# Moving a layer's tail into the next stage, a wait for padding to its reader, and a queue's loads to other places

## The reference

```python
x = _L0(x, ctx, mask)      # cross attention, 16 heads of 16, gated residual
x = _L1(x, ctx)            # RWKV block: recurrence over tokens, 32 heads of 8, then a channel mix
x = _L2(x, ctx, mask)      # grouped-query attention, 32 query heads, 8 key/value heads of 8
x = _L3(x, ctx, ctx)       # two wide cross attentions (16 heads of 128) and an MLP of 1024
```

```python
out = out @ Wo + bo
x = out + hidden_state
mu = jnp.mean(x, axis=-1, keepdims=True)
var = jnp.var(x, axis=-1, keepdims=True)
return (x - mu) * jax.lax.rsqrt(var + EPS) * gamma + beta
```

## Time and profile before

| | |
|---|---|
| median of 3 runs | 1333.27 us (1333.21 to 1338.27) |
| profiled execution, its own time | 1336.37 us |
| span of the profile | 1334.6 us |
| PE busy | 1229.8 us (92%) |
| DVE busy | 807.0 us (60%) |
| ACT busy | 536.7 us (40%) |
| POOL busy | 180.2 us (13%) |
| mean granted TensorE clock | 0.96 |

### The profile page before, as it was taken

The page is one execution under the profiler, slowest core; times in us unless marked ns, Lnnn a source line. Parts: engine busy times, 40 slices in busy tenths (PEclk is TensorE's granted clock), DMA queues, the critical chain, the costliest instruction groups (busy, mean ns, idle before and its releaser), DMA issues.

```text
span 1334.6 us, 17906 instructions
## 1 busy us (share of the span) xinstructions
PE 1229.8 (92%) x6056; PEld 862.5 (65%) x6064; DVE 807.0 (60%) x2386; ACT 536.7 (40%) x1233; POOL 180.2 (13%) x397
## 2 busy tenths in 40 slices
PE   7769788898989787999999699999999999999999
PEld 4347555464555343444443488888888888888887
DVE  4434337586958336787785466666666666666620
ACT  3235343343534324555455343344343434334432
POOL 3122013022212111102011100000000000000000
PEclk9779899899989879999999899999999999999999
DMA  7454623101111535543524733030303030500000
GB/s 224 129 146 127 199 74 117 71 32 64 40 56 49 151 134 153 175 130 118 170 77 140 255 130 119 9 127 0 127 0 127 0 127 0 190 1 1 1 9 24
DMA packets 100652, 127.59 MB, mean 96 GB/s; under 512 B 6737, under 2 KB 78577, under 8 KB 98321
## 3 DMA queue, kind: packets, MB, share of 16 engines
q1 hardware_dynamic: 99936, 126.14, 29.1%
q10 hardware_dynamic: 624, 0.30, 0.1%
HBM read 79.33 MB, written 46.79 MB: 95 GB/s over the span
## 4 chain that ended last, share of the span: by engine, by line
PE 77%; DMA 8%; DVE 5%; ACT 3%; SPq 2%; issue 2%; POOL 2%; ACTq 0%; POOLq 0%; DVEq 0%
PE J L2448 8%; PE J L2466 8%; PE TT L2456 8%; PE S L2422 4%; PE OO L1077 4%; PE TT L2432 4%; PE OO L2422 4%; PE OO L1074 3%; PE J L324 2%; PE J L1077 2%; PE J L1343 2%; PE OO L2666 2%; PE S L634 2%; DMA km<-query_parts 2%; PE J L1074 2%
## 5 line engine op out<-in xcount | busy, mean ns | idle before, releaser
L2524 ACT ACTIVATE PT<-TT 128x512 f32<-128x512 f32 x128 | 76.5, 597 | 281.2 <-PE TT L2432 281.2
L2595 DVE TENSOR_SCALAR QK<-J,cols 128x256 f32<-128x256 f32 x126 | 61.0, 484 | 69.6 <-PE J L2448 69.6
L2559 POOL COPY On<-probs 128x8 f32<-128x8 f32 x128 | 29.1, 227 | 475.3 <-DVE probs L2584 446.0
L2584 DVE TENSOR_SCALAR probs<-probs,inv 128x257 f32<-128x257 f32 x256 | 79.1, 352 | 4.5
L1077 PE MATMUL OO<-ctxT,weights_a 128*128 128x512 f32 x136 | 69.9, 638 | 12.3 <-SPq L308 9.5
L2432 PE MATMUL TT<-ident,probs 128*128 128x128 f32 x512 | 76.9, 273 | 1.7 <-DVE probs L2584 1.7
L1074 PE MATMUL OO<-weights_a,ctxT 128*128 128x512 f32 x136 | 67.8, 622 | 9.8 <-SPq L308 6.1
L2432 PEld LDWEIGHTS TT<-ident,probs 128*128 128x128 f32 x512 | 63.8, 141 | 15.7 <-DVE probs L2584 3.0
L2590 DVE COPY km<-TT 128x256 f32<-128x256 f32 x128 | 54.2, 423 | 31.0 <-PE TT L2456 30.8
L970 DVE CUSTOM_DVE_ANT_0 mask_b<-S,weights_a 128x256 f32<-128x256 f32 x64 | 24.6, 422 | 70.0 <-PE S L634 69.8
L2576 DVE TENSOR_REDUCE maxes<-S 128x1 f32<-128x257 f32 x128 | 48.4, 420 | 30.4 <-PE S L2422 30.4
(11 more groups left out here) (413 smaller groups left out, 2704.4 us busy)
## 6 DMA issues: line engine op xcount, KB each, us to landing
wide_keys<-weights_a SPq DMA_DIRECT2D x64, 256.0 KB, 2.1
wide_values<-weights_a SPq DMA_DIRECT2D x56, 256.0 KB, 2.0
query_parts<-weights_a SPq DMA_DIRECT2D x48, 192.0 KB, 2.8
weights_a<-wide_keys SPq DMA_DIRECT2D x16, 512.0 KB, 7.2
weights_a<-wide_values SPq DMA_DIRECT2D x16, 512.0 KB, 8.4
early<-wide_keys SPq DMA_DIRECT2D x16, 512.0 KB, 8.2
early<-wide_values SPq DMA_DIRECT2D x16, 512.0 KB, 8.7
weights_a<-key_parts SPq DMA_DIRECT2D x16, 288.0 KB
```

Source lines behind the costliest of these rows:

```text
L2524: act.activation(PT[:, n % 2, :], T0[:, :], ACT.Copy).then_inc(pt3_ready, 1)
L2584: ins = dve.tensor_scalar(P_[n % 2][:, qt, :], P_[n % 2][:, qt, :], inv[:, qt, n % 32:n % 32 + 1], None, ALU.mult)
L2595: dve.tensor_scalar(QK[:, n % 2, 0, 0:S], J0[:, 0:S], head_cols(f"bq{a + 1}")[:, h:h + 1], float(DIM3) ** -0.5, ALU.add, ALU.mult).then_in ...
```

## The change

1. The tail of L2's last batch leaves stage 2. PE projects it into bank J1 in place of O0. In the wide stream DVE starts with the two additions, takes statistics and variance at item 0 and centres at item 1; POOL takes the root at item 1, applies gamma at item 2 and beta at item 3. PE's first `add_head`, which overwrites J1, waits for the first addition (`last2_read`), and DVE waits for beta at item 7, before `xn` is written again.
2. PE no longer waits for `pad_ready`; DVE waits for it just before `fetch_values(0)`.
3. In the first layer the copies of step 3 are issued at `at == 1`, with no wait for maxima and so directly behind those of step 2.
4. The table `later` is put in another order: nothing at step 0; mixing weights from step 1 on; `L2_o` and the `rows` table at step 5, ahead of the eight L1 weights, which go to steps 5 to 7. The wait for the eight stores moves with them to `L2_o`.

```diff
--- before.py
+++ after.py
@@ -581,9 +581,11 @@
                 n, i = at // CHUNKS0, at % CHUNKS0
                 b = n // 2
                 if i == 5 and 0 <= n + 1 < STEPS0:
-                    if n < 1:
+                    if n < 0:
                         sp.wait_ge(max0_rows_ready, n + 2)
                         spread0(sp, n + 3)
+                if at == 1:
+                    spread0(sp, 3)
                 if n >= 0 and i >= 6:
                     load_rest(n, 2 * (i - 6), 2 * (i - 6) + 2)
                 if n == 4:
@@ -1432,7 +1434,6 @@
                             pe.wait_ge(max_rows_ready, n + 2)
                         flip_on(n - 1, J0)
 
-                pe.wait_ge(pad_ready, 1)
                 for at in range(-LEAD2, LAST):
                     n, i = at // CHUNKS2, at % CHUNKS2
                     if at >= 0:
@@ -1468,7 +1469,7 @@
                 flip_od(STEPS2 - 1, T0)
                 flip_on(STEPS2 - 1, T1)
                 project_head(pe, 0, 1, 1)
-                project_out(B - 1, O0)
+                project_out(B - 1, J1)
                 bias_rows_pe(pe, 0, S0)
                 meet(pe, "pe")
 
@@ -1608,8 +1609,6 @@
                         front_pool_first(3, pool, 0)
                 pool.wait_ge(max_taken, STEPS2 * SLOTS2)
                 bias_rows_pool(pool, 0)
-                root(B - 1)
-                scale_out(B - 1)
                 meet(pool, "pool")
 
             def dve_program(dve):
@@ -1683,7 +1682,6 @@
                 def centre_out(b):
                     centre(dve, lambda t: xn[:, t, :], xn, own_rstd, rstd2_ready, b + 1, normed2)
 
-                dve.wait_ge(pad_ready, 1)
                 for at in range(-LEAD2, LAST):
                     n, i = at // CHUNKS2, at % CHUNKS2
                     if at == 0:
@@ -1693,6 +1691,7 @@
                     for m, f in fills_of(at):
                         take_maxima(m, f)
                     if at == 2 - LEAD2:
+                        dve.wait_ge(pad_ready, 1)
                         fetch_values(0)
                     if n % 2 == 0 and i == 2 and n // 2 + 1 < B and n >= 0:
                         fetch_values(n // 2 + 1)
@@ -1715,10 +1714,6 @@
                 fetch_q(dve, 0, 0, 0)
                 dve.wait_ge(x_flipped, 1)
                 fetch_q(dve, 0, 1, 1)
-                add_out(B - 1, O0)
-                add_bias()
-                variance()
-                centre_out(B - 1)
                 meet(dve, "dve")
 
             programs["pe"].append(pe_program)
@@ -2385,6 +2380,8 @@
         q3_done, q3_ready = names3("q3_done"), names3("q3_ready")
         var3_ready, rstd3_ready, xn3_ready = names3("var3_ready"), names3("rstd3_ready"), names3("xn3_ready")
         h3_flipped, h3_ready, weights_cleared = names3("h3_flipped"), names3("h3_ready"), names3("weights_cleared")
+        last2_read, last2_var, last2_rstd, last2_normed, last2_step, last2_scaled = (names3(n) for n in (
+            "last2_read", "last2_var", "last2_rstd", "last2_normed", "last2_step", "last2_scaled"))
         FRONT_AT = 8
         ROWS_AT = 3 * HEADS3 + 12
 
@@ -2462,6 +2459,8 @@
                     pe.wait_ge(av3_ready, n + 1)
                     if h == 0 and g >= 1:
                         pe.wait_ge(out3_fetched, g)
+                    if n == 0:
+                        pe.wait_ge(last2_read, 1)
                     for qt in range(TQ):
                         pe.matmul(J1[:, qt * S:(qt + 1) * S], avT[:, n % 2, qt * P:(qt + 1) * P], wide[a][1][:, h, :],
                                   start=(h == 0 and qt == 0), stop=False)
@@ -2560,6 +2559,16 @@
                         .then_inc(weights3_ready, 1)
                     if h == 6:
                         take_root(pool, next_rstd.rearrange("p t o -> p (t o)"), var3_ready, rstd3_ready, g + 1)
+                    if n == 1:
+                        take_root(pool, own_rstd.rearrange("p t o -> p (t o)"), last2_var, last2_rstd, 1)
+                    if n == 2:
+                        gamma = row("L2_xattn_gamma").unsqueeze(1).to_broadcast([P, TQ, C])
+                        pool.wait_ge(last2_normed, 1)
+                        pool.tensor_tensor(xn[:, :, :], xn[:, :, :], gamma, ALU.mult).then_inc(last2_step, 1)
+                    if n == 3:
+                        beta = row("L2_xattn_beta").unsqueeze(1).to_broadcast([P, TQ, C])
+                        pool.wait_ge(last2_step, 1)
+                        pool.tensor_tensor(x_of(B - 1), xn[:, :, :], beta, ALU.add).then_inc(last2_scaled, 1)
                     if n == HEADS3:
                         bias_rows_pool(pool, 1)
                     if h == 0 and g in (B - 1, B):
@@ -2605,6 +2614,10 @@
                     dve.wait_ge(out3_fetched, g + 1)
                     dve.tensor_tensor(x_of(g % B), x_of(g % B), xs[:, :, :], ALU.add)
 
+                bo2 = row("L2_xattn_bo").unsqueeze(1).to_broadcast([P, TQ, C])
+                dve.tensor_tensor(xn[:, :, :], two(J1), x_of(B - 1), ALU.add).then_inc(last2_read, 1)
+                dve.wait_ge(last2_read, 1)
+                chain.link(dve.tensor_tensor(xn[:, :, :], xn[:, :, :], bo2, ALU.add))
                 maxima(0)
                 divide(0)
                 for n in range(ITEMS3):
@@ -2621,6 +2634,13 @@
                         divide(n + 1)
                     if h == 2 and g >= 1:
                         add_out(g - 1)
+                    if n == 0:
+                        take_stats(dve, chain, lambda t: xn[:, t, :])
+                        take_variance(dve, chain, EPS2, own_rstd, last2_var)
+                    if n == 1:
+                        centre(dve, lambda t: xn[:, t, :], xn, own_rstd, last2_rstd, 1, last2_normed)
+                    if n == 7:
+                        dve.wait_ge(last2_scaled, 1)
                     following = x_tok, (g + 1) % B
                     if h == 4:
                         take_stats(dve, chain, tile_of(*following))
@@ -2784,9 +2804,10 @@
             layer1 = load_layer1(split_k)
             table = (rows[:, :, :], "rows", "rows", d["rows"].rearrange("(o r) n -> o r n", o=1)
                      .to_broadcast([P, len(ROWS), C]))
-            later = {0: [table] + layer1[8:11], 1: layer1[11:15], 2: layer1[15:17],
-                     3: [(w[n], n, "w2", split_k(d[n])) for n in ("L2_q", "L2_k", "L2_v", "L2_o")],
-                     5: layer1[0:4], 6: layer1[4:8]}
+            later = {1: layer1[8:12], 2: layer1[12:16],
+                     3: [layer1[16]] + [(w[n], n, "w2", split_k(d[n])) for n in ("L2_q", "L2_k", "L2_v")],
+                     5: [(w["L2_o"], "L2_o", "w2", split_k(d["L2_o"])), table] + layer1[0:2], 6: layer1[2:6],
+                     7: layer1[6:8]}
 
             def load_rest(n, first, last):
                 for dst, name, group, source in later.get(n, [])[first:last]:
@@ -2794,7 +2815,7 @@
                         sp.wait_ge(w2_cleared, 1)
                     if name == "L2_q":
                         sp.wait_ge(ahead_done, FIRST)
-                    if name == "L1_r":
+                    if name == "L2_o":
                         for stored_ in ahead_stored:
                             sp.wait_ge(stored_, 16 * FIRST // 2)
                     load(dst, name, group, source)
```

## The result

The changed kernel takes 1326.4 us (median of 9 runs, 1322.47 to 1330.7) where the kernel before takes 1334.87 us on the same chip (9 runs, 1332.53 to 1340.93): a ratio of 0.993, with a 95% interval of 0.9908 to 0.9953, or some 9.3 us less. The profiled execution took 1327.49 us, its span is 1325.7 us and its mean granted clock 0.961.

A forecast was written before the change was run, and what follows sets the result against it. With TensorE busy for 92% of the span, time could only come from its idle or half-clock places. Tail -4.9, padding -1.9 and first layer -1.0 sum to -7.8 us: 1325.5 us, forecast's own range 1321 to 1329, outer bounds 1315 to 1334.5.

The forecast's parts named there:

- The tail: Last batch's closing work moved from stage 2 into the wide stream: -4.9 us, between -3.5 and -6.0.
- Border: Between stage 2 and the wide stream: GpSimd no longer arrives last, ScalarE's L462 does, 4.6 us earlier.
- The clock's term: First logits of the wide stream: at full speed up to 1.0 us comes back; 0.8 taken.
- DVE's term: Wide stream, items 0 and 1: moved statistics and centring, nearly hidden once; +0.5 us taken, bounds 0 and 1.9.
- the tail gives next to nothing: Rival, chance 0.04: the stream waits for its kept keys instead; tail -1.2 us, sum -4.1, 1329.2 us.
- The padding: Start of stage 2: PE no longer waits for GpSimd's memsets, 1.5 us plus 0.4 of clock: -1.9 us, -1.0 to -3.0.
- The first layer: Step 4 4.5 us sooner, half clock +2.5, step 7's row of maxima +1.0: -1.0 us, between -9 and +5.
- What lies ahead of 82.71: First layer, before batch 2's query writes: company for step 2's copies and step 1's maxima; 3.0 of 0 to 6 us.
- The rows of maxima of steps 1 and 7: First layer: small transfers slowed by traffic; 0 to 3 us more at step 1, 0 to 5 at step 7.
- The rival that rests on them: Chance 0.06: both rows about 5 us late with half clock behind; layer +16, sum +9.2, 1342.5 us.
- The queue's order: Rival, first layer, chance 0.20: step 2 not delayed, step 1's small row slips in; layer -6, sum -12.8, 1320.5 us.
- The stall only changes its place: Rival, first layer, chance 0.20: both delays near upper ends, half clock after step 4; layer +4, sum -2.8, 1330.5 us.

The follow-up runs named there:

- the split: Each half's key copies issued as three copies of 24 rows: 1307.09 us, ratio 0.9799, on the changed kernel; 1315.5 us, 0.9853, on the kernel before.

## Why the prediction was right, and where it was off

The forecast of 1325.5 us met 1326.4 us, and its sum of -7.8 us met -9.3 us (-12.3 to -6.3). Part by part, from the profiles:

- **The tail** (forecast -4.9 us). Border -4.67 us, as against -4.6. The opening of the stream was forecast as +0.5 for DVE and -0.8 for the clock, -0.3 together; the stream takes either 518.49 or 519.86 us in the eight profiles with the new tail, against 519.15 us in all but one of the others: -0.66 or +0.71 us. Together -5.3 or -4.0 us; the time of this part alone, -3.2 (-5.9 to -0.7) us, agrees. The clock's term is there: the first flip comes 0.88 us sooner after the first logits. DVE's term did not come as named. The wait of 1.97 us in item 0 is in all eight profiles, to 0.01 us, and lies ahead of the moved statistics; in five of them the stream ends 0.66 us shorter, so that additions, statistics and centring cost at most 0.2 us. In the other three, this change's among them, the clock falls to half behind that wait for some 4 us. That costs 1.4 us more, the whole difference between the two lengths. The prediction has no such term. The rival "the tail gives next to nothing" is out by the profiles: its waiting for kept keys is not there, and the first logits start 1.17 us after L462. The time alone would not exclude its -1.2 us.
- **The padding** (forecast -1.9 us). Stage 2 is 2.2 us shorter by the means over 14 profiles. PE starts with the memsets, as forecast.
- **The first layer** (forecast -1.0 us, -9 to +5). The signs that were named came: no stall before step 3, 7.13 us before step 4 (forecast 9), six query writes in 3.16 us (forecast 3.2), half clock behind step 4. Three terms of the sum were too small. What lies ahead of 82.71 cost 4.0 us (86.73) where 3.0 were taken: 1.36 us of later landing, then half clock until 72. From the last write's issue to the copy under way it was 4.45 us and not 3.9. The set of step 4, itself with company, took 13.40 us and not 12.2. So step 4 started at 107.79 and not at 105.0, only 1.75 us sooner than before. The half clock behind it cost 2.9 us (2.5 taken): matched matmul by matmul, the changed kernel is 1.1 us behind the one before at 113.74. The rows of maxima of steps 1 and 7 have no idle time here (1.0 us taken for step 7), but the term is not empty: the kernel with both edits of the first layer alone waits 1.15 us for the row of step 7, the one that holds step 3 back 1.72 us, and that one also 1.14 us for the row of step 1. The rival that rests on them (1342.5 us) is out for this kernel. By its own terms the layer's sum is thus +1.1 us and not -1.0. Two things that the sum does not have come on top in this profile: from 138 to 158 us the clock is at half, which costs 7.5 us and comes in place of the 4.21 us of waiting at 154.44 and the half clock behind it; and in the last matmuls, from 192 to 196 us, the clock is 1.00 where the kernel before has 0.57, which brings the layer back to -0.07.
- **The queue's order.** By it step 2 is not delayed. It was, by 1.36 us; with the copies of step 3 held back, it was at 66.45 in place of 67.58. That rival (1320.5 us) is out as it was built. The Trainium skill's rule that a DMA engine takes one issuer's descriptors in ring order ("DMA: Bandwidth & Descriptors", section "Queues, rings and completion order") does not by itself keep a set's time: 12.85 us against 11.23 us here.
- **The stall only changes its place** came nearest of the rivals in the first layer's mechanism: in the one pair of profiles the layer's end moved by 0.07 us. But the edits to the layer have layer ends of 197.22 and 193.54 us, mean 195.4, against 197.7 us for the three profiles with the old layer. That is -2.3 us, on a spread of 2 to 4 us, and the forecast's -1.0 lies within it; so does the time of the two edits alone, -0.7 us (-2.8 to +1.6). The rival's sum of -2.8 us lies outside the interval of the whole.
- **The value and the reason.** That 1325.5 met 1326.4 to 0.9 us is in part luck: the border and the padding are shown at their size, but the layer's sum is 2.1 us off by its own terms, the stream has two lengths 1.4 us apart, and a stage without a changed line differs by 5 us. The pair of profiles agrees with the forecast in its sum, -8.9 us, by other terms: -5.0 us of it stands in the recurrent layer, which nobody changed. Among the kernels that leave out padding, tail or both, it takes 279.65 to 284.31 us (seven profiles, mean 282.7), and among those with both 278.92 to 283.84 us (seven, mean 280.1). Whether the change brings on the shorter one or meets it more often by chance is open: the times of the whole change and of its parts differ by 2 us in the sum, which is where it would have to show, and the intervals are wider.

What the prediction did not see is that the sets themselves were the thing to change. Its rows had it: a fifth of the DMA engines' time at 78 GB/s, which it read as a price for company; and the chain of the earlier trace rows has one more set that it passed over, step 0's, 12.63 us from 27.01, with PE idle for 4.50 us before 39.68. The Trainium skill's "DMA: Bandwidth & Descriptors", section "Why a DMA increments its semaphore by 16 and not by 1", gives a broadcast with a slowest dimension of three only three engines; that the split removed the share of 0.19 and took the set from 11 to 13 us down to 8 us agrees with it. How many engines a copy uses was not read from a trace.

## What to carry to other kernels

When a long stall is taken from a chain of transfers, follow the chain to the next consumer before counting the gain: here 10.8 us of stall came back as 7.1 us one step later. A DMA share that stays low and flat for many microseconds while something waits can be a transfer with too few engines at work, and splitting it can be worth more than any order of the queue: here 16.4 us against none that the times show. A longer wait at one place is not yet a price: match the instructions of both kernels and see whether the work behind the wait starts later, and at which clock. And in a kernel whose unchanged stages differ by 5 us from one profile to the next, a part of 1 to 2 us is settled by the same stage over many profiles, not by one pair and not by the total time.

## What the hardware showed that was not expected

- Two DMA issues took 5.32 us on the sync engine with one set and the keys of a second already on their way, and 0.87 us without; with the keys split, the same two issues took 0.81 us behind as many bytes.
- A step's keys in six DMAs in place of two, with the same bytes, made its set land in 8.0 us and not in 11.2 to 13.4 us, though the issues themselves grew from 1.45 us to 2.4 us for the keys of a step.
- Code that is the same differs by the clock it is granted. The stream takes 518.49 us (five profiles) when the clock stays whole behind the wait of 1.97 us in its item 0, and 519.86 us (three) when it falls to 0.50 there. The recurrent layer takes 278.9 to 279.7 us in six profiles and 281.9 to 284.3 us in eight, with a granted clock of 1.00 or 0.83 in the same 20 us of one profile each. What decides whether the clock falls was not found.
